# Six image buffers in the two attention passes, the maxima's rows first in the queue, and another TensorE order in the embedding

## What is computed

```
tokens = concat(cls, patches @ W_map.T + b_map) + positions      # per image: 197 x 192
x      = (tokens - mean) / sqrt(var + eps) * ln_w + ln_b         # mean and var over the whole image
q,k,v  = per-head 16x16 products of x, 12 heads
h      = tokens + softmax(q k' / 4) v                            # attention 1, not causal
h      = norm(h + attention2(h, W_qkv, W_out, b_out))            # attention 2, causal
h      = norm(h + soft_mixture_of_64_experts(h))                 # route, experts, combine
```

## Time and profile before

| | |
|---|---|
| time, median of 3 runs | 5207.82 us (5204.32 to 5209.99) |
| the profiled execution | 5199.24 us, span 5197.5 us, clock 0.953 |
| embedding | from 0 to about 1028 us |
| attention 1 | about 1028 to 2769 us |
| attention 2 | about 2769 to 4155 us |
| route, experts, combine | to 5197.5 us |
| busy over the span | TensorE 88%, VectorE 58%, ScalarE 53%, GpSimd 51% |
| transfers | 789.87 MB, mean 152 GB/s |

### The profile page before, as it was taken

The page is one execution under the profiler, slowest core; times in us unless marked ns, Lnnn a source line. Parts: engine busy times, 40 slices in busy tenths (PEclk is TensorE's granted clock), DMA queues, the critical chain, the costliest instruction groups (busy, mean ns, idle before and its releaser), DMA issues. The chain is left out here.

```text
span 5197.5 us, 159359 instructions
## 1 busy us (share of the span) xinstructions
PE 4585.4 (88%) x48245; PEld 3916.5 (75%) x48311; DVE 3025.4 (58%) x8734; ACT 2768.0 (53%) x6788; POOL 2665.6 (51%) x4485
## 2 busy tenths in 40 slices
PE   7999999789999999999997999999999888889975
PEld 7888888767777777777775777777777666668953
DVE  3444444466666666666665666666666589980048
ACT  3334343356666666665663555555555467773446
POOL 2333333345555555555554666666666568881125
PEclk9999999989999999999998999999999889999975
DMA  6777777667777777777765666666666423329988
GB/s 156 177 178 176 177 177 178 158 131 149 149 153 152 149 150 151 150 153 152 149 142 114 135 131 132 132 130 134 133 133 133 88 83 93 93 79 257 276 238 260
DMA packets 692799, 789.87 MB, mean 152 GB/s; under 512 B 362225, under 2 KB 514767, under 8 KB 692720
## 3 DMA queue, kind: packets, MB, share of 16 engines
q1 hardware_dynamic: 692720, 788.90, 66.4%
HBM read 519.30 MB, written 265.72 MB: 151 GB/s over the span
## 5 line engine op out<-in xcount | busy, mean ns | idle before, releaser
L738 DVE TENSOR_REDUCE a_mx<-a_sq 99x2 f32<-99x394 f32 x1536 | 798.3, 561 | 515.5 <-PE a_sq L788 515.2
L738 DVE TENSOR_REDUCE c_mx<-c_sq 99x2 f32<-99x198 f32 (+1 forms) x1536 | 642.0, 459 | 310.2 <-PE c_sq L788 310.0
L679 ACT ACTIVATE a_ex<-a_sk 99x792 f32<-99x792 f32 (+1 forms) x768 | 638.5, 832 | 231.1 <-PE a_sk L810 185.3
L679 ACT ACTIVATE c_ex<-c_sk 99x792 f32<-99x792 f32 (+1 forms) x768 | 512.0, 667 | 243.1 <-PE c_sk L804 172.9
L601 POOL TENSOR_SCALAR_AFFINE_SELECT c_ex<-c_ex 99x396 f32<-99x396 f32 (+1 forms) x768 | 418.8, 550 | 291.5 <-ACT c_ex L679 288.1
L365 PE MATMUL e_tokp<-e_wmap,e_ptT 128*99 128x192 f32 x3072 | 543.9, 327 | 21.3 <-DVE e_cvar L323 21.3
L810 PE MATMUL a_sk<-a_qs,a_ks 99*99 99x198 bf16 (+1 forms) x3072 | 427.0, 262 | 98.4 <-DMA a_qs<-a_mxp 98.3
L365 PEld LDWEIGHTS e_tokp<-e_wmap,e_ptT 128*99 128x99 f32 x3072 | 482.7, 167 | 21.6 <-issue 21.3
L788 PE MATMUL a_sq<-a_ks,a_qs 96*99 96x198 bf16 x3072 | 453.7, 261 | 40.1 <-DVE a_wl L723 25.1
L810 PEld LDWEIGHTS a_sk<-a_qs,a_ks 99*99 99x99 bf16 (+1 forms) x3072 | 295.3, 130 | 241.3 <-issue 237.0
L275 POOL CAST e_parts<-e_rest 96x396 bf16<-96x396 f32 x256 | 131.0, 512 | 651.7 <-DVE e_rest L345 651.7
(11 more groups left out here) (196 smaller groups left out, 11614.9 us busy)
## 6 DMA issues: line engine op xcount, KB each, us to landing
e_ptT<-in_x SPq DMA_DIRECT2D x128, 594.0 KB
x_w<-in_fc SPq DMA_DIRECT2D x128, 576.0 KB, 5.9
scr_qk<-e_parts SPq DMA_DIRECT2D x128, 445.5 KB
scr_qk<-a_parts SPq DMA_DIRECT2D x128, 445.5 KB
scr_tv<-e_tv SPq DMA_DIRECT2D x128, 297.0 KB
a_tv<-scr_tv SPq DMA_DIRECT2D x128, 297.0 KB
scr_tv<-a_res SPq DMA_DIRECT2D x128, 297.0 KB
c_tv<-scr_tv SPq DMA_DIRECT2D x128, 297.0 KB
```

The source lines that it names most:

```text
L679: nc.scalar.activation(to, of, ACT.Exp).then_inc(exped.sem, 1)
L738: nc.vector.reduce_max(mx[:, b2.parity, qt, h:h + 2], sq[f % 2][:, :, 0:width], AX.X).then_inc(maxed.sem, 1)
```

## The change

In `embed_pass` TensorE's step begins with the first half of the token product; then come the sum, the transposes, the second half of the token product, q, the variance, k and v. ScalarE's and VectorE's steps are put in an order that fits: the copy L297 first, the root L300 between q and k, the tokens' sum L351 before the rests of q and k. No work is added or taken out, and the number of buffers stays.

In `attend_pass` R is 6 (six buffers of qs, ks, tv and vx, and six steps in a turn of the loop), `res` and `parts` have three buffers, and SP's step begins with the three rows of maxima, before the stores. The constants are set by GpSimd (the three rows of `ks` as 4-byte elements, two bf16 ones each), the weights are loaded after the loads of images 0 and 1 and split by VectorE at the start of its step 4, and TensorE waits for constants and weights only in the steps that first use them. In the diff, lines that only put `third` for `parity` or 3 for 2 are cut to examples.

```diff
-                    act.wait_ge(x_turned.sem, x_turned.at(b3))
-                    nc.scalar.copy(xT[0:CH, b3.parity], xtp[:]).then_inc(x_copied.sem, 1)
-                if b2.inside(n):
-                    act.wait_ge(var_p.sem, var_p.at(b2))
-                    nc.scalar.activation(st[:, b2.place, 4:5], varp[:, 0:1], ACT.Sqrt, bias=eps[:, 0:1]).then_inc(std.sem, 1)
...
+                for i, (done, p) in enumerate(((q_done, qp), (k_done, kp))):
+                    if b3.inside(n):
                         act.wait_ge(done.sem, done.at(b3))
                         split_high(nc.scalar, parts[:, b3.place, i, :, place_of(i, 0)], p[:], SCALES[i]).then_inc(high.sem, 1)
+                    if i == 0 and b2.inside(n):
+                        act.wait_ge(var_p.sem, var_p.at(b2))
+                        nc.scalar.activation(st[:, b2.place, 4:5], varp[:, 0:1], ACT.Sqrt, bias=eps[:, 0:1]).then_inc(std.sem, 1)
+                if b3.inside(n):
                     act.wait_ge(v_done.sem, v_done.at(b3))
                     nc.scalar.copy(tv[:, b3.place, 1], vp[:]).then_inc(v_copied.sem, 1)
...
+                if b1.inside(n):
+                    dve.wait_ge(embedded.sem, embedded.at(b1))
+                    dve.wait_ge(stored.of(b1 - 4), stored.at(b1 - 4))
+                    nc.vector.scalar_tensor_tensor(out=tv[:, b1.place, 0], in0=tokp[b1.parity][:], scalar=1.0, in1=posb[:],
+                                                   op0=ALU.mult, op1=ALU.add,
+                                                   accum_out=st[:, b1.place, 0:1]).then_inc(tokens.sem, 1)
+                if b3.inside(n):
+                    left_of(b3, 0, qp)
...
                 b1, b2, b3 = c - 1, c - 2, c - 3
+                if b1.inside(n):
+                    pe.wait_ge(loaded.of(b1), loaded.at(b1))
+                    pe.wait_ge(tokens.sem, tokens.at(b1 - 2))
+                    token_tile(b1, 0)
                 if b2.inside(n):
                     pe.wait_ge(tokens.sem, tokens.at(b2))
                     pe.wait_ge(mean_s.sem, mean_s.at(b2 - 1))
...
                 if b1.inside(n):
-                    pe.wait_ge(loaded.of(b1), loaded.at(b1))
-                    pe.wait_ge(tokens.sem, tokens.at(b1 - 2))
-                    token_tile(b1, 0)
-                if b2.inside(n):
-                    pe.wait_ge(squares.sem, squares.at(b2))
-                    pe.wait_ge(std.sem, std.at(b2 - 1))
-                    for t in range(2):
-                        mm = nc.tensor.matmul(varp[:, 0:1], cvar[:, t], st[:, b2.place, 2 + t:3 + t],
-                                              start=(t == 0), stop=(t == 1))
-                    mm.then_inc(var_p.sem, 1)
+                    token_tile(b1, 1).then_inc(embedded.sem, 1)
                 if b3.inside(n):
                     pe.wait_ge(x_copied.sem, x_copied.at(b3))
-                    for i, (done, p) in enumerate(((q_done, qp), (k_done, kp))):
+                for i, (done, p) in enumerate(((q_done, qp), (k_done, kp))):
+                    if b3.inside(n):
                         pe.wait_ge(left.sem, left.at(b3 - 1, i + 1))
                         for h in range(2):
                             mm = nc.tensor.matmul(p[:, h], wqkv[:, i, h], xT[:, b3.parity, h], start=True, stop=True)
                         mm.then_inc(done.sem, 1)
+                    if i == 0 and b2.inside(n):
+                        pe.wait_ge(squares.sem, squares.at(b2))
+                        pe.wait_ge(std.sem, std.at(b2 - 1))
+                        for t in range(2):
+                            mm = nc.tensor.matmul(varp[:, 0:1], cvar[:, t], st[:, b2.place, 2 + t:3 + t],
+                                                  start=(t == 0), stop=(t == 1))
+                        mm.then_inc(var_p.sem, 1)
+                if b3.inside(n):
                     pe.wait_ge(v_copied.sem, v_copied.at(b3 - 1))
                     for t in range(2):
                         for h in range(2):
                             mm = nc.tensor.matmul(vp[:, t, h * CH:(h + 1) * CH], xT[:, b3.parity, h, t * TT:(t + 1) * TT],
                                                   wqkv[:, 2, h], start=True, stop=True)
                     mm.then_inc(v_done.sem, 1)
-                if b1.inside(n):
-                    token_tile(b1, 1).then_inc(embedded.sem, 1)
             pipeline(pe, n, DEPTH, R, step)
 
 
 def attend_pass(nc, n, A, scr, causal):
-    R = 4
+    R = 6
     DEPTH = 7
...
-        res = m.sb(X + "res", [TT, 2, 2, 2, D])
+        res = m.sb(X + "res", [TT, 3, 2, 2, D])
...
-        n_const, n_ready = (4 * 16, 9) if causal else (2 * 16, 5)
+        n_const = (3 if causal else 1) * 16
...
-            loads = [(ident[:], A["ident"])]
+            sp.dma_start(ident[:], A["ident"]).then_inc(const, 16)
             if causal:
-                loads += [(w[:], A["wout"].rearrange("(c p) d -> p c d", p=CH)), (bout[:, 0], A["bout"]), (mask[:, 0], A["above"])]
-            else:
-                loads += [(w[:], A["wqkv2"].rearrange("(c p) d -> p c d", p=CH))]
-            for to, of in loads:
-                sp.dma_start(to, of).then_inc(const, 16)
-
-            def step(c):
-                b = c - 7
-                if b.inside(n):
-                    sp.wait_ge(finished.sem, finished.at(b))
-                    if causal:
-                        sp.dma_start(scr["h_pre"][b.number].rearrange("(t p) d -> p t d", p=TT), res[:, b.parity, 0]).then_inc(stored.of(b), 16)
-                    else:
-                        sp.wait_ge(added.sem, added.at(b))
-                        sp.dma_start(scr["tv2"][b.number], res[:, b.parity]).then_inc(stored.of(b), 16)
-                        sp.wait_ge(q_low.sem, q_low.at(b))
-                        sp.wait_ge(k_low.sem, k_low.at(b))
-                        sp.dma_start(scr["qk2"][b.number].rearrange("i c a p s -> p (i c a) s"),
-                                     parts[:, b.parity].rearrange("p i c a s -> p (i c a) s")).then_inc(stored.of(b), 16)
+                sp.dma_start(mask[:, 0], A["above"]).then_inc(const, 16)
+                sp.dma_start(bout[:, 0], A["bout"]).then_inc(const, 16)
+
+            def step(c):
                 b = c - 3
                 if b.inside(n):
                     sp.wait_ge(max_low.sem, max_low.at(b))
                     for a in range(PARTS):
                         sp.dma_start(qs[STACK + a:STACK + a + 1, b.place], mxp[:, b.parity, a]).then_inc(max_in_place.of(b), 16)
+                b = c - 7
+                if b.inside(n):
+                    sp.wait_ge(finished.sem, finished.at(b))
+                    if causal:
+                        sp.dma_start(scr["h_pre"][b.number].rearrange("(t p) d -> p t d", p=TT), res[:, b.third, 0]).then_inc(stored.of(b), 16)
+                    else:
+                        sp.wait_ge(added.sem, added.at(b))
+                        sp.dma_start(scr["tv2"][b.number], res[:, b.third]).then_inc(stored.of(b), 16)
+                        sp.wait_ge(q_low.sem, q_low.at(b))
+                        sp.wait_ge(k_low.sem, k_low.at(b))
+                        sp.dma_start(scr["qk2"][b.number].rearrange("i c a p s -> p (i c a) s"),
+                                     parts[:, b.third].rearrange("p i c a s -> p (i c a) s")).then_inc(stored.of(b), 16)
                 b = c - 1
                 if b.inside(n):
-                    sp.wait_ge(added.sem, added.at(b - 4))
-                    sp.wait_ge(v_spread.sem, v_spread.at(b - 4))
+                    sp.wait_ge(added.sem, added.at(b - R))
+                    sp.wait_ge(v_spread.sem, v_spread.at(b - R))
                     sp.dma_start(tv[:, b.place], tv_in[b.number]).then_inc(tv_in_place.of(b), 16)
                 if c.inside(n):
-                    sp.wait_ge(scored_k.sem, scored_k.at(c - 4))
+                    sp.wait_ge(scored_k.sem, scored_k.at(c - R))
...
+                if c.is_number(1):
+                    sp.dma_start(w[:], A["wout" if causal else "wqkv2"].rearrange("(c p) d -> p c d", p=CH)).then_inc(weighed, 16)
...
-            pool.wait_ge(ready, n_ready)
+            pool.memset(vx[:], 0.0).then_inc(zeroed, 1)
+            pool.wait_ge(zeroed, 1)
+            pool.memset(vx[:, :, :, :, DH:DH + 1], 1.0).then_inc(vx_ones, 1)
+            pool.wait_ge(vx_ones, 1)
+            pool.memset(ks[STACK:AUG].rearrange("p r h s -> p (r h s)").bitcast(F32), ONE_TWICE).then_inc(ks_ones, 1)
+            pool.wait_ge(ks_ones, 1)
+            if causal:
+                pool.wait_ge(ready, 4)
...
                         pool.wait_ge(o_normed.sem, o_normed.at(b5))
-                        pool.wait_ge(stored.of(b5 - 2), stored.at(b5 - 2))
-                        pool.tensor_tensor(res[:, b5.parity, 0], tv[:, b5.place, 0], on[:, b5.parity],
+                        pool.wait_ge(stored.of(b5 - 3), stored.at(b5 - 3))
+                        pool.tensor_tensor(res[:, b5.third, 0], tv[:, b5.place, 0], on[:, b5.parity],
...
```

(49 more changed lines are left out.)

40 lines of the change are left out of this document (19 added, 21 removed).

## The result

The changed kernel takes 5346.23 us (median of 4 runs, 5340.39 to 5362.89), the kernel before 5208.9 us on the same chip. The ratio is 1.0255, with a 95% interval of 1.0206 to 1.0303: slower by 2.6%, where 4934 us was forecast, faster by 5%. The profiled execution has a span of 5338.7 us at a mean granted clock of 0.913. The experiments ran at other times, on more than one chip, where the kernel before took 5184 to 5207 us, so each is given as a ratio to the kernel before, run beside it. One run of the first experiment, 5181.52 us at a granted clock of 0.891, fell into a slower state; it is in that experiment's median and in no ratio.

A forecast was written before the change was run, and what follows sets the result against it. TensorE bounds the kernel; its idle tenth is mainly one wait per pass. 5197.5 - 110 (embedding) - 151 (attention 1) - 2 (attention 2) - 11 (starts) = 4923.5 us span; with 1.7 and 8.6 added, 4934, range 4905 to 5050.

The forecast's parts named there:

- the price of instruction fetch at the loop's turn: Attention passes: if six steps' code is not kept, each of 2 x 20 turns fetches again; 1.2 to 7.1 us each.
- the two chances: Attention loops: 0.11 for fetch at 3 us a turn (5054 us), 0.03 for slower than before (5294 at 9 us).
- the rival's own sum: Attention loops: forecast 4934 us plus the fetch at 40 turns, 120 us at 3 us each, so 5054; chance 0.11.
- 0.86 for that: Chances of cases without refetch: forecast 0.70, a wait that stays 0.10, unchanged attention 1 0.05, no difference 0.01.
- Embedding: Embedding pass: the wait before L374 goes, pitch from 7.74 to 6.87 us, a gain of 110 us.
- Attention 1: First attention pass: the wait for the rows of maxima goes, pitch from 13.21 to 11.99 us, gain 151 us.
- the whole sum of 4934 us: Whole kernel: span 4923.5 us after all gains, with 1.7 and 8.6 us added; chance 0.70.
- the starts: Start of both attention passes: first products 7.5 and about 6.5 us earlier, gain 11 us for both, ends +15 and -11.
- the two buffers, not SP's order: Attention 1: two buffers of `res` make late stores delay GpSimd's L650 and the next burst; rows land 0.99 us late.
- Rows first alone would change little: Attention 1: putting the rows first in SP's step alone changes little, since SP wasn't held by the stores.
- the 15.3 us estimated: Attention starts: time for GpSimd to set the constants of vx and ks, from about 1028 to 1044, hidden, just.
- the copy's 1.31: Attention starts: ns per element from GpSimd's copy of 384 in 502 ns, used to price its constants.

The follow-up runs named there:

- the first experiment: The changed kernel with R = 4 instead of 6 and four buffers instead of three for `res` and `parts`: 4916.49 us, ratio 0.9473.

## Why the prediction was wrong

**The step that failed** is the price of instruction fetch at the loop's turn, and with it the two chances. The mechanism was named, with the right number of turns (2 x 20). The length was put at 7.0 packets, from packets that were mostly those of steps written out; the loops are 7.5 and 6.9. A fetch was given a chance of 0.11 at 3 us a turn, and 0.03 at over 6.9 us, the point from which it decides. The runs show 10.1 us. At that price the rival's own sum is 4934 + 404 = 5338, and 5346 was measured. The argument against it was that a packet per 10 us is little and that TensorE can be sent the next while it works. Both hold for code without a loop, as the run with the steps written out shows; neither holds at a jump back, where TensorE stands still until a packet is there (stalls of 3.12 and 4.02 us, one packet in each). The price was bounded by transfers of data, 1.2 to 7.1 us for one wait. But a turn has two waits (3.12 and 4.02 us), and behind them a stretch at the lower clock. Of 406 us lost, 291 are waited. The rest is mostly in longer instructions: in attention 1 a product of TensorE takes 1575.20 / 18275 = 86.2 ns here, and 1467.11 / 17792 = 82.5 ns in the first experiment. The bounds for this rival were for one wait, and the value taken, 3 us, was near the lower of them.

The trace of before said that its loop of four steps is kept, and nothing of six. That was no evidence that six are kept, and 0.86 for that was too much. The Trainium skill's rule on the two-page window (Runtime: NRT & Kernel Launch, Instruction fetch mechanics), weighed in the prediction, would have a fetch at each turn of either loop. The kernel before, and the loops up to 6.7 packets, show none, so for TensorE the window is wider here. The same section of the Trainium skill gives TensorE 128 KiB, eight packets; that the prediction took as room for its seven, and neither loop of the changed kernel (7.5 and 6.9) was kept.

**What held.** Embedding: forecast 6.87 us a step, measured 6.78; the wait is gone, the gain 121.5 us instead of 110. Attention 1: forecast 11.99, measured 11.94 inside a turn and 11.94 in both runs without the stalls, four steps and written out; in the first of them TensorE has the full clock and the transfers a share of 0.78. Taken without the fetch, the whole sum of 4934 us, 0.947 of the median, is the 0.9473 and 0.9476 measured. That it fits so closely is partly luck: the embedding gave about as much more than its term as the starts gave less than theirs.

**That it is the two buffers, not SP's order,** held: the buffers alone give 0.943. "Rows first alone would change little" was wrong. It left out that the stores then stand behind the rows, and that two buffers make GpSimd wait for just these stores. What is queued behind the moved step, and who waits for that, should have been counted.

**The starts.** First products: forecast near 8 us after SP's first issue, measured 914.43 - 906.01 = 8.4, where it was 15.4, and 9.6 in attention 2, where it was 14.8. But a gain of 11 us in all was credited, and none shows. GpSimd's constants, which the trace of before had no row for, cost less than the 15.3 us estimated (shortest, median and longest in ns, and where it starts):

```profile
L593 POOL MEMSET a_vx<- x1: 3939/3939/3939, 905.5 to 905.5; 99x4608 f32 x1
L595 POOL MEMSET a_vx<- x1: 338/338/338, 909.5 to 909.5; 99x144 f32 x1
...
L597 POOL MEMSET a_ks<- x1: 6037/6037/6037, 909.9 to 909.9; 3x7128 f32 x1
```

Together they are 10.3 us. That is 0.86 ns for an element of the first, nearer to the 0.83 that the prediction worked out from the Trainium skill (GPSIMD Engine Reference, Performance versus the Vector engine) than to the copy's 1.31, which the sum went by.

## What to carry to other kernels

A number of buffers that is also the number of steps in a loop's turn has a price in code, and that price is a step function: count the instruction packets of the longest engine's turn, in the loop and not written out, before adding steps, and separate the two numbers or write the loop out where the length grows. When a step is put ahead of another in a queue, follow what is now behind it round to the step itself: with too few buffers that ring sets the pitch. And an earlier first product is no gain until the first steady image is earlier.

## What the runs showed of the hardware

- TensorE kept a loop of 6.7 packets of 16 KB (110 KB) and didn't keep one of 6.9 (113 KB) or one of 7.5. Some 9 and 10 packets come for each turn of these two.
- Each such turn costs 10.1 us with this kernel's transfers at a share of 0.70, in one or two stalls, 7.3 us together on average and 7.4 for the longest single one, and a stretch at the lower clock.
- Code without a jump costs nothing: 133 packets in 1400 us, and a pitch that is the same to 0.02 us.
- Two waits that are true at once make one instruction, by the profile's counts.
- The same step takes 23 to 24 instructions of TensorE more in a loop than written out.
- With the same start of attention 1 TensorE left 1.2 GHz at 939 us in one trace and at 952 in another; an earlier first product didn't bring that forward.
